# Edge gathers of a graph network kernel: one gather issued ahead of the wait for the preceding pair

## The chip, the core and the metric

The kernel runs on one core of one Trainium2 chip. Its time is the device time of one execution in microseconds; lower is better. "GB/s" and "us" below are those of the profile.

## The reference

One message passing layer with a residual and a layer norm, over 12,500 nodes of 64 features and 212,500 edges of 32 features, sorted by destination, all float32:

```python
msg_in = concatenate([nodes[row], nodes[col], edge_features])
messages = relu(msg_in @ mW1 + mb1) @ mW2 + mb2
aggregated = segment_sum(messages, col, num_segments=nodes.shape[0])
upd_in = concatenate([nodes, aggregated])
out = relu(upd_in @ uW1 + ub1) @ uW2 + ub2
result = layernorm(x + out)          # eps = 1e-5
```

`row` is the source of an edge, `col` its destination.

## The kernel before, in words

The source part of the message is linear ahead of the relu, so a first stage multiplies all nodes with the source rows of `mW1` and writes the product to a table in HBM, `table_src` (12,500 rows of 128 float32, 512 bytes each). The main loop then goes over the edges in 208 *pairs* p = 0 to 207. A pair is 1,024 edges in eight tiles of 128; the last is shorter. Each pair uses one of four slots, k = p mod 4, of every buffer. The sequence of a pair, by engine:

- **SyncE** (`load_two`, L636 and L639; `load_window`, L657) loads edge features (256 KB) and destination numbers, broadcast over 96 partitions (768 KB), for two pairs at a time, and a window of 96 destination nodes for each pair. A load waits for `pe_steps`, TensorE's count of steps that are over.
- **GpSimd** (`step`, L785 to L797) issues one indirect DMA for each tile: 128 rows of `table_src`, chosen by the source numbers in `idx_all`, 64 KB, into `gath` at slot k. Even pairs have eight gathers. Odd pairs from 11 on have seven: their eighth tile gets its source columns from ScalarE and VectorE instead (`col_x`, L516 and L539). Pairs 0 to 5 are gathered in another form, before the loop (L779). Each gather raises `gathered[k]` by 16 when it has landed.
- **TensorE** (`pre`, L912) multiplies the edges' features and a one-hot of their destinations into `ps_pre`; later (`summing`, L932) it adds the relu of the pair into the sums of 96 nodes, after which `window` (L845) prepares a window and ends the step (`pe_steps`).
- **VectorE** (`add_gathered`, L1298) adds `gath` to `ps_pre`, giving `hid`, and raises `hsum_made`; it waits for `pe_steps` and for `gathered[k]`. Its other work for a pair is the one-hots (L1261), `turned` (L1269) and the sums' ring (L1324, L1325).
- **ScalarE** takes the relu (L1103), copies 60 columns for each second pair (L516), and copies the window (L1065).

From pair 24 on, node work of 49 blocks of 256 nodes goes between, one block for four pairs (TensorE L979 to L995, ScalarE L1152 to L1160, VectorE L1402, output by L1164).

GpSimd's order is the program's own. Ahead of a pair's gathers `step` has up to four things: for p of 10 or more the wait that pair p-4 has been added (`hsum_made`, which frees the slot of `gath`), for p = 16 a wait for the rest of the index table, for p of 7 or more the wait that all gathers of pair p-1 have landed (`gathered[(k - 1) % SLOTS]`), and `let`, which raises a semaphore that nobody reads, so that the waits sit on an instruction of their own. `RAW` is 6, `SLOTS` 4, `EARLY` 16.

Of the kernel before, what the change touches and what calls it, by code (L numbers as in the profile page):

```python
# [41 lines left out]
SLOTS = 4  # L42
# [31 lines left out]
RAW = 6  # L74
# [46 lines left out]
def gnn_kernel(nc, x, xT, srcT, dst, dstT, edgeT, mW1, mb1, mW2T, mb2, uW1, ub1, uW2, ub2, out):  # L121
# [4 lines left out]
    with ExitStack() as ctx:  # L126
# [6 lines left out]
        def sem(name):  # L133
            return ctx.enter_context(nc.semaphore(name))
# [146 lines left out]
        gathered = [sem(f"gathered{i}") for i in range(SLOTS)]  # L281
# [44 lines left out]
        def let(eng):  # L326


            eng.sem_inc(passed, 1)
# [19 lines left out]
        def pair(it, k, back=0):  # L349

            it, k = it + (k - back) // SLOTS, (k - back) % SLOTS
            p = it * SLOTS + k
            return None if isinstance(p, int) and not 0 <= p < PAIRS else (p, it, k)

        def is_last(p):

            return isinstance(p, int) and p == LAST_PAIR
# [11 lines left out]
        def parts(p):  # L369

            return ((0, TILES, P), (TILES, 1, TAIL)) if is_last(p) else ((0, PT, P),)

        def tiles_of(p):

            return [(first + j, m) for first, t, m in parts(p) for j in range(t)]

        def rows_of(p):


            return LAST_ROWS if is_last(p) else PT  # L380
# [58 lines left out]
        def is_raw(p):  # L439

            return isinstance(p, int) and p < RAW
# [5 lines left out]
        def has_cols(p):  # L447

            return COL_FROM <= p < PAIRS and (p - COL_FROM) % COL_EVERY == 0
# [5 lines left out]
        def gathers_of(p):  # L455

            return rows_of(p) if is_last(p) else PT - has_cols(p)

        def got(p):


            return 16 * sum(gathers_of(q) for q in range(RAW, p + 1) if q % SLOTS == p % SLOTS)
# [87 lines left out]
        def src_by_tile(p, j, m):  # L550

            return bass.IndirectOffsetOnAxis(ap=idx_all[0:m, p * PT + j:p * PT + j + 1], axis=0)
# [198 lines left out]
        def _(pool):  # L751
# [33 lines left out]
            def step(it, k):  # L785
                p, it, k = pair(it, k)
                if is_raw(p):
                    return
                if p >= RAW + SLOTS:
                    pool.wait_ge(hsum_made, p - SLOTS + 1)  # L790
                if p == EARLY:
                    pool.wait_ge(idx_last_in, 16)
                if p > RAW:
                    pool.wait_ge(gathered[(k - 1) % SLOTS], got(p - 1))
                let(pool)
                for j, m in tiles_of(p)[0:gathers_of(p)]:
                    pool.indirect_dma_start(gath[0:m, k, j * H:(j + 1) * H], None, table_src, src_by_tile(p, j, m)).then_inc(gathered[k], 16)  # L797

            with pool.If(fit == 1):
                pool.wait_ge(idx_rest_in, 16)  # L800
                pairs(pool, step, lambda *chunk: None, lambda i: None)
# [698 lines left out]
```

## Time and profile before

| | |
|---|---|
| median of 3 runs | 2489.68 us (2489.13 to 2490.9) |
| the profiled execution | 2490.1 us |
| its span, first to last instruction | 2488.3 us |
| mean granted TensorE clock | 0.72 |
| busy: TensorE, GpSimd, VectorE, ScalarE | 62%, 59%, 45%, 39% |

The span is what the profile's rows cover; the time is 1.8 us more. In a group of instructions "busy" is the sum of their durations, and "idle" is how long their engine had nothing running before them, with what ended most of it. A releaser "issue" means that the profile shows nothing that the engine waited for; a GpSimd pause with that releaser can still be a wait, since semaphore instructions have no rows. A gather's duration is the generation of its descriptors, not the movement of its data.

### The profile page before, as it was taken

What the parts mean: (1) busy time and instruction counts of PE and PEld (TensorE: products, weight loads), DVE (VectorE), ACT (ScalarE), POOL (GpSimd) and SP (SyncE); (2) the same over time, 40 slices, a digit from 0 to 9 for tenths busy, and PEclk for the clock granted to TensorE, in tenths of its full rate; (3) what the DMA queues carried; (4) which work ended last, traced back from release to release, by engine and by line L of the source; (5) the groups of instructions that cost most, each with busy time, mean ns of one, the idle gap of its engine ahead of it and who ended that gap; (6) DMA issues with size and microseconds to landing.
All of it is one profiled execution on the core that took longest, in us unless ns stands there. A gap on an engine that the chain in (4) does not pass through costs nothing. (4 is left out here: it accounts for less than half of the span.)

```text
span 2488.3 us, 35326 instructions
## 1 busy us (share of the span) xinstructions
PE 1553.6 (62%) x8744; PEld 1428.1 (57%) x8744; DVE 1114.3 (45%) x4860; ACT 972.5 (39%) x6697; POOL 1475.7 (59%) x1576
## 2 busy tenths in 40 slices
PE   2676666665666666576666666567566566557657
PEld 2566655555565565565565565556566555556555
DVE  3435445444444444444444444444444444444443
ACT  1215334334334434443433433443433444443342
POOL 7155566666656666566666565665656666666653
PEclk6787776776766866766767777776766777676776
DMA  4634434333334333333333343343333343333331
GB/s 109 179 91 108 98 81 99 97 85 92 98 80 98 97 90 90 96 96 83 97 94 85 95 99 83 95 99 80 97 96 85 93 99 94 84 98 93 86 91 33
DMA packets 102736, 232.74 MB, mean 94 GB/s; under 512 B 47018, under 2 KB 63223, under 8 KB 89917
## 3 DMA queue, kind: packets, MB, share of 16 engines
q1 hardware_dynamic: 42532, 124.03, 19.9%
q0 software_dynamic: 49952, 100.83, 16.4%
q10 hardware_dynamic: 10046, 5.59, 0.9%
q8 instruction: 75, 1.23, 0.2%
q14 instruction: 131, 1.07, 0.2%
HBM read 220.66 MB, written 9.60 MB: 93 GB/s over the span
## 5 line engine op out<-in xcount | busy, mean ns | idle before, releaser
L797 POOL DMA_INDIRECT gath<-table_src,idx_all x1513 | 1427.6, 944 | 970.9 <-issue 873.0
L932 PE MATMUL ps_sum<-onehot,hid 128*128 128x96 f32 x3322 | 598.4, 353 | 628.0 <-ACT rhs L1065 535.8
L932 PEld LDWEIGHTS ps_sum<-onehot,hid 128*128 128x128 f32 x3322 | 563.4, 263 | 664.2 <-issue 659.8
L516 ACT COPY col_x<-xz 64x1 f32 x5960 | 634.9, 187 | 409.5 <-issue 403.9
L912 PE MATMUL ps_pre<-rhs,lhs 128*128 128x128 f32 x3226 | 593.7, 360 | 222.6 <-issue 164.3
L1298 DVE TENSOR_TENSOR hid<-ps_pre,gath 128x1024 f32<-128x1024 f32 x202 | 246.7, 1221 | 1067.3 <-DMA gath<-table_src,idx_all 925.6
L912 PEld LDWEIGHTS ps_pre<-rhs,lhs 128*128 128x128 f32 x3226 | 560.6, 270 | 244.1 <-issue 179.4
L1103 ACT ACTIVATE hid<-hid 128x1024 f32<-128x1024 f32 x202 | 212.7, 1053 | 358.9 <-DVE hid L1298 356.1
L539 DVE TENSOR_TENSOR col_x<-xz 64x2 int32 x3366 | 265.2, 148 | 81.5 <-issue 78.6
L1269 DVE TENSOR_SCALAR_CACHE_REDUCE lhs<-lhs,place 96x1024 f32<-96x1024 int32 x208 | 262.6, 1263 | 62.9 <-PE ps_sum L845 32.5
L1261 DVE TENSOR_TENSOR onehot<-ps_iota,dst_rel 128x768 f32<-128x768 f32 (+1 forms) x209 | 196.8, 942 | 0.1
L1065 ACT COPY rhs<-ps_sum 96x128 f32<-96x128 f32 x208 | 53.4, 258 | 307.6 <-issue 254.8
L1152 ACT ACTIVATE late_b<-ps_node,ub1c 128x256 f32<-128x256 f32 x47 | 22.3, 474 | 288.5 <-PE ps_node L985 270.1
L934 PE MATMUL ps_sum<-ident,deg 96*128 96x96 f32 x416 | 107.4, 350 | 2.5 <-issue 2.5
L845 PE MATMUL ps_sum<-w_dst,xwin 65*96 65x128 f32 x416 | 98.7, 324 | 9.7 <-DMA xwin<-in_xT_dram 9.7
L934 PEld LDWEIGHTS ps_sum<-ident,deg 96*128 96x128 f32 x416 | 89.1, 263 | 4.2 <-issue 4.1
L845 PEld LDWEIGHTS ps_sum<-w_dst,xwin 65*96 65x96 f32 x416 | 63.9, 189 | 23.3 <-DMA xwin<-in_xT_dram 10.1
L871 PE MATMUL ps_pre<-w_src,xz 128*128 128x128 f32 (+1 forms) x200 | 30.4, 321 | 60.4 <-ACT gath L1072 29.8
L871 PEld LDWEIGHTS ps_pre<-w_src,xz 128*128 128x128 f32 (+1 forms) x200 | 29.1, 231 | 61.2 <-issue 60.9
L1325 DVE TENSOR_TENSOR xz<-xz,ps_sum 1x96 f32 x208 | 54.2, 261 | 6.4
L919 PE MATMUL ps_pre<-w_src,col_x 64*128 64x128 f32 x200 | 53.4, 350 | 0.0
L1324 DVE TENSOR_TENSOR agg<-agg,ps_sum 128x96 f32 x208 | 50.6, 243 | 1.7 <-PE ps_sum L934 1.6
(136 smaller groups left out, 672.6 us busy)
## 6 DMA issues: line engine op xcount, KB each, us to landing
lhs<-in_dst_dram SPq DMA_DIRECT2D x99, 768.0 KB
lhs<-in_edgeT_dram SPq DMA_DIRECT2D x98, 256.0 KB
gath<-table_src,idx_all POOLq DMA_INDIRECT x1513
table_src<-gath SPq DMA_DIRECT2D x12, 512.0 KB, 5.3
xwin<-in_xT_dram SPq DMA_DIRECT2D x208, 24.0 KB
lhs<-in_dst_dram SPq DMA_DIRECT2D x10, 384.0 KB
out_dram<-late_b ACTq DMA_DIRECT2D x48, 64.0 KB, 2.7
xz<-in_xT_dram ACTq DMA_DIRECT2D x4, 512.0 KB, 5.1
```

The source lines that it names most:

```text
L516: ins = copy(col_x[:, k, start + n + j:start + n + j + 1], col)
L539: ins = nc.vector.tensor_tensor(to[:, at:at + 2].bitcast(I32), first, second, ALU.bitwise_or)
L797: pool.indirect_dma_start(gath[0:m, k, j * H:(j + 1) * H], None, table_src, src_by_tile(p, j, m)).then_inc(gathered[k], 16)
L845: return nc.tensor.matmul(win(p, k), xwin[:, k, :], w_dst[:, :], start=True, stop=True)
L871: mm = nc.tensor.matmul(ps_pre[q % 2][0:m, j * H:(j + 1) * H], xz[0:kk, of], w[0:kk, :], start=True, stop=True)
L912: mm = nc.tensor.matmul(to[0:m, j * H:(j + 1) * H], lhs[:, k, j * P:j * P + m], rhs[:, k, :], start=True, stop=not by_cols)
L932: nc.tensor.matmul(bank[:, 0:WIN], hid[0:m, k, j * H:(j + 1) * H], hot(k, j, m), start=(j == 0), stop=(m == TAIL or j == PT - 1))
L934: return nc.tensor.matmul(bank[:, P:P + WIN], deg[0:WIN, k:k + 1].broadcast_to([WIN, P]), ident[0:WIN, 0:WIN], start=True, stop=True)
L1103: nc.scalar.activation(h, h, ACT.Relu).then_inc(hid_made, 1)
L1261: ins = nc.vector.tensor_tensor(to, nums.broadcast_to([m, t, WIN]), at.broadcast_to([m, t, WIN]), ALU.is_equal)
L1269: nc.vector.tensor_scalar(whole, whole.bitcast(I32), place[0:WIN, cols(p, 1)], 0.0, ALU.is_equal, ALU.add, accum_out=deg[0:WIN, k:k + 1]). ...
L1298: nc.vector.tensor_tensor(hid[:, k, at], ps_pre[k % 2][:, at], gath[:, k, at], ALU.add).then_inc(hsum_made, 1)
```

## The change

In GpSimd's `step` the wait for pair p-1's gathers no longer stands ahead of the loop over the tiles but inside it, ahead of the second gather. An extra `let` goes with it.

```diff
@@ -790,10 +790,11 @@
                     pool.wait_ge(hsum_made, p - SLOTS + 1)
                 if p == EARLY:
                     pool.wait_ge(idx_last_in, 16)
-                if p > RAW:
-                    pool.wait_ge(gathered[(k - 1) % SLOTS], got(p - 1))
                 let(pool)
-                for j, m in tiles_of(p)[0:gathers_of(p)]:
+                for n, (j, m) in enumerate(tiles_of(p)[0:gathers_of(p)]):
+                    if n == 1 and p > RAW:
+                        pool.wait_ge(gathered[(k - 1) % SLOTS], got(p - 1))
+                        let(pool)
                     pool.indirect_dma_start(gath[0:m, k, j * H:(j + 1) * H], None, table_src, src_by_tile(p, j, m)).then_inc(gathered[k], 16)
```

The order of GpSimd's instructions at pairs 10 and 11 (slots 2 and 3), before:

```order
L797 DMA gath<-table_src,idx_all 128x128 [waits hsum_made,gathered1]
L797 DMA gath<-table_src,idx_all 128x128 x7
L797 DMA gath<-table_src,idx_all 128x128 [waits hsum_made,gathered2]
L797 DMA gath<-table_src,idx_all 128x128 x6
L797 DMA gath<-table_src,idx_all 128x128 [waits hsum_made,gathered3]
```

Each pair's first gather waits for both. The same place with the change:

```order
L798 DMA gath<-table_src,idx_all 128x128 [waits hsum_made]
L798 DMA gath<-table_src,idx_all 128x128 [waits gathered1]
L798 DMA gath<-table_src,idx_all 128x128 x6
L798 DMA gath<-table_src,idx_all 128x128 [waits hsum_made]
L798 DMA gath<-table_src,idx_all 128x128 [waits gathered2]
L798 DMA gath<-table_src,idx_all 128x128 x5
L798 DMA gath<-table_src,idx_all 128x128 [waits hsum_made]
```

The wait for the sums has stayed at the first gather, and the wait for the preceding pair's gathers is at the second. On the other engines nothing moves but line numbers, by one.

## Rows read from the trace of the kernel before

**Rows 1.** The page: its span, and section 1, busy time of each engine.

```profile
span 2488.3 us, 35326 instructions
...
PE 1553.6 (62%) x8744; PEld 1428.1 (57%) x8744; DVE 1114.3 (45%) x4860; ACT 972.5 (39%) x6697; POOL 1475.7 (59%) x1576
```

**Rows 2.** The page's costliest groups: busy, mean ns | idle before, releaser.

```profile
L797 POOL DMA_INDIRECT gath<-table_src,idx_all x1513 | 1427.6, 944 | 970.9 <-issue 873.0
...
L1298 DVE TENSOR_TENSOR hid<-ps_pre,gath 128x1024 f32<-128x1024 f32 x202 | 246.7, 1221 | 1067.3 <-DMA gath<-table_src,idx_all 925.6
```

**Rows 3.** Timeline of GpSimd, pairs 82 to 84: start, duration, work [idle before].

```profile
1011.41 0.95 POOL L797 DMA_INDIRECT gath<-table_src,idx_all  x1 [2.44 <-issue]
1012.66 0.94 POOL L797 DMA_INDIRECT gath<-table_src,idx_all  x1 [0.30 <-issue]
...
1020.17 0.94 POOL L797 DMA_INDIRECT gath<-table_src,idx_all  x1 [0.30 <-issue]
1023.44 0.94 POOL L797 DMA_INDIRECT gath<-table_src,idx_all  x1 [2.32 <-issue]
...
1034.28 0.94 POOL L797 DMA_INDIRECT gath<-table_src,idx_all  x1 [2.40 <-issue]
```

**Rows 4.** Timeline of other engines at the pause before pair 83.

```profile
1020.49 0.46 PE L845 MATMUL ps_sum<-w_dst,xwin 65*96 65x128 f32 x2
...
1022.77 1.23 DVE L1298 TENSOR_TENSOR hid<-ps_pre,gath 128x1024 f32<-128x1024 f32 x1 [6.23 <-DMA gath<-table_src,idx_all]
1022.93 0.32 SPq L636 DMA_DIRECT2D lhs<-in_edgeT_dram  x1
```

**Rows 5.** Timeline of GpSimd: first and last of 15 long pauses, pairs 33 and 201.

```profile
444.23 0.94 POOL L797 DMA_INDIRECT gath<-table_src,idx_all  x1 [4.58 <-issue]
...
2390.97 0.94 POOL L797 DMA_INDIRECT gath<-table_src,idx_all  x1 [4.57 <-issue]
```

**Rows 6.** Timeline of the early loop: pair 10's first gather, L1298 of pairs 11, 16.

```profile
170.19 0.94 POOL L797 DMA_INDIRECT gath<-table_src,idx_all  x1 [10.58 <-DVE hid L1298]
...
212.35 1.23 DVE L1298 TENSOR_TENSOR hid<-ps_pre,gath 128x1024 f32<-128x1024 f32 x1 [0.49 <-issue]
...
257.09 1.23 DVE L1298 TENSOR_TENSOR hid<-ps_pre,gath 128x1024 f32<-128x1024 f32 x1
```

**Rows 7.** Timeline of ScalarE over four pairs, without the column copies.

```profile
998.93 1.06 ACT L1103 ACTIVATE hid<-hid 128x1024 f32<-128x1024 f32 x1 [0.48 <-DVE hid L1298]
...
1010.97 0.25 ACT L1065 COPY rhs<-ps_sum 96x128 f32<-96x128 f32 x1
1012.00 1.06 ACT L1103 ACTIVATE hid<-hid 128x1024 f32<-128x1024 f32 x1 [0.79 <-DVE hid L1298]
...
1024.03 1.06 ACT L1103 ACTIVATE hid<-hid 128x1024 f32<-128x1024 f32 x1 [6.39 <-DVE hid L1298]
...
1035.97 1.06 ACT L1103 ACTIVATE hid<-hid 128x1024 f32<-128x1024 f32 x1
...
1045.91 0.47 ACT L1152 ACTIVATE late_b<-ps_node,ub1c 128x256 f32<-128x256 f32 x1 [6.09 <-PE ps_node L985]
```

**Rows 8.** Pauses that met a load, the loads, and two stretches (DMA share, GB/s last).

```profile
187.50 0.32 SPq L636 DMA_DIRECT2D lhs<-in_edgeT_dram  x1
...
196.57 0.94 POOL L797 DMA_INDIRECT gath<-table_src,idx_all  x1 [4.86 <-issue]
...
225.35 0.32 SPq L636 DMA_DIRECT2D lhs<-in_edgeT_dram  x1
...
233.65 0.95 POOL L797 DMA_INDIRECT gath<-table_src,idx_all  x1 [4.58 <-issue]
...
261.86 0.32 SPq L636 DMA_DIRECT2D lhs<-in_edgeT_dram  x1
...
270.57 0.94 POOL L797 DMA_INDIRECT gath<-table_src,idx_all  x1 [5.49 <-issue]
...
1000.00:1004.00 4.00, 3.00 (x26) 3.00 (x26) 2.63 (x20) 3.80 (x40) 2.83 (x3) 1.00 0.95 223
1006.00:1010.00 4.00, 0.00 (x0) 0.00 (x0) 0.00 (x0) 1.60 (x12) 2.37 (x3) 0.59 0.21 61
```

**Rows 9.** The chain that ended last: landing after the last gather.

```profile
2462.01 2.56 DMA gath<-table_src,idx_all
```

## The prediction

> **What bounds the kernel now.** I read the page first: its span and busy shares [rows 1]. No engine is near full: TensorE shows 62%, GpSimd 59%. So a wait sets the pace, and the costliest groups say which [rows 2]. VectorE's addition at L1298, the first reader of the gathered rows, spent 1067 us idle before its 202 instructions, 926 of them ended by the gathers' landing. GpSimd's own gathers, 1513 of 944 ns, had 971 us of idle time before them.
>
> The timeline of GpSimd shows how that idle time is made [rows 3]. Eight gathers of pair 82 start between 1011.41 and 1020.17, seven steps of 1.25 us (0.94 busy, 0.30 between). Then comes 2.32 us of nothing, and the first gather of pair 83 at 1023.44: 12.03 us from pair to pair. Pair 83 has seven gathers and takes 10.84 us (to 1034.28). The second half of the reading is who woke at that pause [rows 4]: the last gather is generated at 1021.12, VectorE's L1298, which waits for the same landing, starts at 1022.77, and GpSimd's next gather 0.67 us behind it. A pause is thus 1.65 us of landing and 0.67 us of restart; both are in the path, since GpSimd waits for the landing before it generates anything. The waits of pairs 7 to 207 are 201; 15 of them, every twelfth pair from 33 to 201, last 4.5 to 4.6 us [rows 5]. Their landing is on time and the restart is 2.2 us late; nothing in the profile says why.
>
> Is anything else as slow? At the start of the loop the gathers are far ahead, and the rest of the kernel runs at its own pace: L1298 of pair 11 at 212.35, of pair 16 at 257.09 [rows 6], so 8.95 us per pair. That is without the node work, which begins at pair 24. So from about pair 17 on, the gather stream bounds the loop with a margin of some 2.5 us per pair.
>
> **The change, part by part.**
>
> *The wait moves behind one gather.* For pair 83 the first gather would start 0.30 us after the last one of pair 82, at 1021.42, and be generated at 1022.37, still before the landing that L1298 sees at 1022.77. The second gather is then released by that landing and starts at 1023.44, where the first one started before. Each pair becomes shorter by one step, 1.25 us. The wait is still there, with about 1.1 us of it uncovered. This holds for the long pauses as well, as long as the pause is over 1.55 us; all are.
>
> *How many pairs count.* The first gather of pair 10 at 170.19 was released by L1298 of an earlier pair, not by a landing [rows 6]. That wait stays ahead of the first gather, so what is won before pair 10 is lost there. Pairs 11 to 207 remain: 197 x 1.25 = 246 us. From pair 11 to 16 the other engines are behind the gathers, and these savings do not show at once; they show when the others have caught up, since the gathers' own line of time keeps them.
>
> *Added instructions.* The wait for the sums used to sit with the wait for the gathers; now it stands alone, with a semaphore increment of its own. It is for the pair four back, whose L1298 was over some three pairs ago, so it waits for nothing. What an extra semaphore step costs has no row. Lower bound 0, since the gap of 0.30 us between gathers is there anyway; upper bound one such gap per pair, 197 x 0.30 = 59 us. I take 0: the 0.67 us of restart contain such a step already, and it now stands ahead of the first gather, where there is slack of 1.1 us before the landing's release.
>
> *What the earlier first gather touches.* Its slot was free since the wait for the sums passed. It puts 64 KB into the DMA queues behind the preceding pair's last gather, and its data moves after that one's. No instruction on SyncE or another queue moves. But the pairs get shorter, and SyncE's loads may meet other gathers. Where a load of 1,024 KB started 3 to 4 us before a pair's last gather was generated, the pause grew from 2.33 to 4.86, 4.58 and 5.49 us [rows 8], by 2.65 us in the mean and 3.16 at most. In steady state the load starts 0.16 us behind L1298 [rows 4], and nobody waits for the gathers that it meets. So a meeting costs between 0 and 3.16 us, and I take 0 for the sum, since the steady rows are the nearest; the rest is a rival.
>
> The Trainium skill (DMA: Bandwidth & Descriptors, "Queues, rings and completion order") says that each DMA engine takes turns between the queues that have work, packet by packet. By that rule a gather would wait for about one packet of the load; as an estimate, 16 x 8 KB at the 223 GB/s of [rows 8] is 0.6 us, and with one meeting in four pairs the time would be 2273. The trace does not agree: its pauses grew four times as much.
>
> *The 15 late restarts* cost 15 x 2.2 = 33 us now. They may fall elsewhere among the shifted instructions: between 0 and 33 us to gain, as much to lose. I take no change.
>
> *The tail.* From the last gather to the end (2462.01 to 2488.3) [rows 9] nothing changes.
>
> Sum: 2490.1 (the profiled execution's own time, 1.8 over its span) - 246 = 2244.1; the median of the runs is 0.4 lower, so 2244.
>
> **The rivals.**
>
> *ScalarE's chain takes over.* ScalarE copies columns for every second pair, and TensorE waits for its window copy (L1065) [rows 7]. From the relu at 998.93 to the next at 1012.00 it is idle for 0.79 us only: 12.3 us for a pair in which the gathers will leave 9.6. The pair after it needs 5.6 (12.0 less 6.4 idle), the next column pair 11.9 (1024.03 to 1035.97), and the fourth 10.4 to the end of L1152, which waits for TensorE. Together 40.2 us per four pairs, against 2 x (12.03 + 10.84) = 45.7 now and 45.7 - 5.0 = 40.7 after. So there is half a microsecond of slack in four pairs, and lateness in a column pair must be made up in the next. A chain longer by 1 to 1.5 us would cost 25 to 50 us over the 49 groups of four: about 2280. For it speaks the small slack, against it that TensorE's part was measured partly at half clock and that it would idle less.
>
> *The loads run into the last gather.* SyncE loads for every second pair, 98 times. TensorE's window matmul that frees the buffer ends at 1020.95, the load follows at 1022.93 [rows 4]. With pairs of 9.6 and 10.8 us the load of the pair behind a late ScalarE step (it came 11.7 us after the window copy's end at 1011.22) would start some 1 to 3 us before the next pair's last gather is generated. If one load of two collides, 49 x 2.65 = 130 us are given back: 2374. Against it speaks that the load keeps to the landing rather than to the matmul: 2 us pass between matmul and load, which no row explains.
>
> *All loads collide: slower.* The same mechanism at both loads of each four pairs. It decides at 246 / 98 loads = 2.5 us each. At 2.65 us the time is 2244 + 260 = 2504, at 3.16 it is 2554. It needs TensorE's steps to be out of step with the landings in both places. The second load would come to an end about 1 us before the last gather's data, by the same reckoning, so I hold this for unlikely.
>
> *Nothing is covered: no change.* If the landing were held up while GpSimd generates, the first gather would only push it back, and the time stays at 2490. Against it: with GpSimd generating and no load running the queues move 61 GB/s [rows 8], no less than the 52 GB/s of one gather's 64 KB per 1.25 us; so gathers land while others are generated.
>
> **How the numbers follow.** Forecast 2244: 0.52. ScalarE's chain, 2280: 0.14. One load of two, 2374: 0.26. All loads, 2504: 0.05. No change: 0.03. The low end takes the late restarts as gone, 2244 - 33 = 2211, and the high end reaches to the third case with its price at 3.16 (2244 + 155 = 2399, cut to 2395). A measurement of this kernel tells 0.2% (5 us) from no change. Faster by more: the first three, 0.92; within: 0.03; slower: 0.05.
>
> **What would show it.** Right: the pause moves between the first and second gather of a pair and is 1.1 us long, the step across the pair boundary is 1.25 us, two pairs take 20.4 us; L1298 still idles before the landing. The ScalarE rival shows as L1298 waiting for something other than the gathers; the load rivals as pauses of 3 to 4 us every fourth (or second) pair with an SP load starting before the last gather. I am wrong if the first gather of a pair is itself delayed, by the wait for the sums or by a longer generation than 944 ns.

## The result and the profile after

In the comparison the changed kernel takes 2838.13 us (median of 4 runs, 2819.52 to 2856.88) and the kernel before 2490.29 (4 runs): ratio 1.139 [1.132, 1.147], slower by 14%, far outside the range of the prediction. This verdict is one chip's. The same two kernels on another chip give 2197.68 against 2517.55, ratio 0.872 [0.868, 0.877]: faster by 13%. How these go together is what most of this text is about.

The page of the changed kernel, with the groups that answer to [rows 1, 2] (busy, mean ns | idle before, releaser), and its chain that ended last:

```profile
span 2855.2 us, 35526 instructions
...
PE 1579.5 (55%) x8744; PEld 1423.7 (50%) x8744; DVE 1134.0 (40%) x4860; ACT 1001.2 (35%) x6697; POOL 1478.1 (52%) x1576
...
another core or an unknown queue 43%; DVE 24%; issue 15%; PE 10%; DVEq 5%; ACT 1%; DMA 0%; SPq 0%; ACTq 0%
...
L798 POOL DMA_INDIRECT gath<-table_src,idx_all x1513 | 1429.9, 945 | 1307.3 <-DVE hid L1299 657.6
...
L516 ACT COPY col_x<-xz 64x1 f32 x5960 | 677.8, 190 | 720.7 <-issue 716.5
...
L1270 DVE TENSOR_SCALAR_CACHE_REDUCE lhs<-lhs,place 96x1024 f32<-96x1024 int32 x208 | 263.8, 1268 | 1298.2 <-remote 1204.0
...
L1299 DVE TENSOR_TENSOR hid<-ps_pre,gath 128x1024 f32<-128x1024 f32 x202 | 246.7, 1221 | 68.4 <-issue 57.0
```

Work has not grown: the gathers are 945 ns each as before, the busy sums are nearly those of [rows 1]. But the direction of waiting has turned. L1299 (before: L1298) idled 1067 us for the gathers [rows 2] and now 68; the gathers idle 1307 us instead of 971, half of it for VectorE's additions (`hid`, L1299), which free a slot of `gath`. VectorE in turn idles 1298 us ahead of `turned` (L1270), for something that the profile can only call remote, and the chain of waits is to 43% "an unknown queue". The kernel before had 63 us ahead of that instruction:

```profile
L1269 DVE TENSOR_SCALAR_CACHE_REDUCE lhs<-lhs,place 96x1024 f32<-96x1024 int32 x208 | 262.6, 1263 | 62.9 <-PE ps_sum L845 32.5
...
L516 ACT COPY col_x<-xz 64x1 f32 x5960 | 634.9, 187 | 409.5 <-issue 403.9
```

The second row, of the kernel before too, did not stand in the prediction and should have: ScalarE's column copies idled 404 us for nothing that the profile shows. Nor did the 44.6 us for which GpSimd idled ahead of the loop's first gather, at 109.07 us; they come up again below.

The timeline of the changed kernel, GpSimd:

```profile
1001.47 0.94 POOL L798 DMA_INDIRECT gath<-table_src,idx_all  x1 [0.30 <-issue]
...
1002.71 0.94 POOL L798 DMA_INDIRECT gath<-table_src,idx_all  x1 [0.30 <-issue]
...
1004.86 0.94 POOL L798 DMA_INDIRECT gath<-table_src,idx_all  x1 [1.20 <-issue]
...
1011.11 0.94 POOL L798 DMA_INDIRECT gath<-table_src,idx_all  x1 [0.30 <-issue]
...
1018.66 0.94 POOL L798 DMA_INDIRECT gath<-table_src,idx_all  x1 [6.61 <-DVE hid L1299]
...
1037.14 0.96 POOL L798 DMA_INDIRECT gath<-table_src,idx_all  x1 [8.79 <-DVE hid L1299]
```

The first pair boundary (1001.47, 1002.71, then the pause of 1.20 ahead of the second gather) is what the prediction drew. What it did not draw are the pauses of 6.6 and 8.8 us. The same stretch on the other engines:

```profile
1001.68 0.19 ACT L516 COPY col_x<-xz 64x1 f32 x1 [0.52 <-issue]
1001.68 0.15 DVE L539 TENSOR_TENSOR col_x<-xz 64x2 int32 x1 [0.56 <-issue]
1001.70 0.37 PE L846 MATMUL ps_sum<-w_dst,xwin 65*96 65x128 f32 x1 [1.86 <-issue]
1002.39 0.19 ACT L516 COPY col_x<-xz 64x1 f32 x1 [0.53 <-issue]
...
1003.09 0.19 ACT L516 COPY col_x<-xz 64x1 f32 x1 [0.51 <-issue]
1003.11 0.37 PE L846 MATMUL ps_sum<-w_dst,xwin 65*96 65x128 f32 x1 [1.05 <-issue]
...
1014.44 2.34 ACT L516 COPY col_x<-xz 64x1 f32 x24 [0.51 <-issue]
...
1014.88 1.27 DVE L1270 TENSOR_SCALAR_CACHE_REDUCE lhs<-lhs,place 96x1024 f32<-96x1024 int32 x1 [9.49 <-remote]
...
1016.65 1.23 DVE L1299 TENSOR_TENSOR hid<-ps_pre,gath 128x1024 f32<-128x1024 f32 x1
...
1019.64 3.81 ACT L516 COPY col_x<-xz 64x1 f32 x38
...
1024.71 0.46 PE L846 MATMUL ps_sum<-w_dst,xwin 65*96 65x128 f32 x2
...
1030.12 0.32 SPq L636 DMA_DIRECT2D lhs<-in_edgeT_dram  x1
```

ScalarE, VectorE and TensorE creep side by side, one instruction each per 0.71 us or a multiple of it, as if taking turns. TensorE's window matmuls (L846) end at 1003.48; VectorE's L1270, which waits for that step's count, starts 11.4 us later. Later the matmul ends at 1025.17 and the load that waits for the same count starts 4.95 us behind it. I call this the *hold*. It is over at 1014.44 (24 copies in 2.34 us, 0.10 each), some 2.4 us after the last gather that GpSimd could issue was generated (1012.05); the next one had to wait for L1299. After the restart at 1018.66 copies run at full speed until 1023.45; then the hold is back.

So it reads as a circle: the sums wait for TensorE's count, the count for a moment in which no gather is under way (I call it a *full stop*), and that moment often comes only when GpSimd has run out of free slots and stands waiting for the sums. In the kernel before every pair ended in such a full stop. There all 92 loads of edge features after 300 us start 1.74 to 1.99 us behind the end of a pair's last gather, which is its landing, and 0.6 to 3.6 us behind the matmul that releases them. With the change 59 of 93 start in a pause of GpSimd's, 30 held ones start while it generates, and 4 are prompt; the longest is 19.4 us behind its matmul. A full stop thus lets the count through, but it is not the only moment at which the count can pass.

### The profile page after: what moved, and what is told of

Read it like the earlier page. It is cut to its first block, busy times and chain, and to the rows that moved or that the text cites. A ratio compares the mean times of both kernels' runs of the same rounds, so it can differ in the third digit from the quotient of the medians.

```text
span 2855.2 us, 35526 instructions
## 1 busy us (share of the span) xinstructions
PE 1579.5 (55%) x8744; PEld 1423.7 (50%) x8744; DVE 1134.0 (40%) x4860; ACT 1001.2 (35%) x6697; POOL 1478.1 (52%) x1576
## 4 chain that ended last, share of the span: by engine, by line
another core or an unknown queue 43%; DVE 24%; issue 15%; PE 10%; DVEq 5%; ACT 1%; DMA 0%; SPq 0%; ACTq 0%
DVE col_x L539 8%; DVE hid L1299 7%; DVEq L500 4%; DVE onehot L1262 4%; PE ps_pre L913 4%; PE ps_sum L933 2%; DVE lhs L1270 2%; DVE xz L1326 1%; PE ps_sum L846 1%; DVE agg L1325 1%; ACT col_x L516 1%; DVEq L1309 1%; PE ps_pre L920 0%; DMA table_src<-gath 0%
## 5 line engine op out<-in xcount | busy, mean ns | idle before, releaser
L913 PE MATMUL ps_pre<-rhs,lhs 128*128 128x128 f32 x3226 | 618.2, 358 | 584.0 <-DVE lhs L1270 370.7
L516 ACT COPY col_x<-xz 64x1 f32 x5960 | 677.8, 190 | 720.7 <-issue 716.5
L1270 DVE TENSOR_SCALAR_CACHE_REDUCE lhs<-lhs,place 96x1024 f32<-96x1024 int32 x208 | 263.8, 1268 | 1298.2 <-remote 1204.0
L933 PE MATMUL ps_sum<-onehot,hid 128*128 128x96 f32 x3322 | 551.9, 331 | 329.5 <-ACT rhs L1066 149.3
L933 PEld LDWEIGHTS ps_sum<-onehot,hid 128*128 128x128 f32 x3322 | 522.7, 244 | 362.0 <-issue 305.6
L539 DVE TENSOR_TENSOR col_x<-xz 64x2 int32 x3366 | 280.7, 148 | 241.1 <-issue 239.2
L1299 DVE TENSOR_TENSOR hid<-ps_pre,gath 128x1024 f32<-128x1024 f32 x202 | 246.7, 1221 | 68.4 <-issue 57.0
L846 PE MATMUL ps_sum<-w_dst,xwin 65*96 65x128 f32 x416 | 110.4, 340 | 82.4 <-issue 72.3
L846 PEld LDWEIGHTS ps_sum<-w_dst,xwin 65*96 65x96 f32 x416 | 68.8, 197 | 96.4 <-issue 75.2
L995 PE MATMUL ps_node<-uw,late_b 128*128 128x64 f32 x188 | 48.2, 312 | 106.7 <-issue 106.7
L995 PEld LDWEIGHTS ps_node<-uw,late_b 128*128 128x128 f32 x188 | 44.1, 263 | 114.5 <-issue 114.4
L996 PE MATMUL ps_node<-cent,xz 65*128 65x64 f32 x188 | 50.3, 335 | 75.7 <-issue 75.7
L996 PEld LDWEIGHTS ps_node<-cent,xz 65*128 65x128 f32 x188 | 44.2, 267 | 86.2 <-issue 86.2
```

What stands on the lines that cost most here:

```text
L516: ins = copy(col_x[:, k, start + n + j:start + n + j + 1], col)
L539: ins = nc.vector.tensor_tensor(to[:, at:at + 2].bitcast(I32), first, second, ALU.bitwise_or)
L846: return nc.tensor.matmul(win(p, k), xwin[:, k, :], w_dst[:, :], start=True, stop=True)
L913: mm = nc.tensor.matmul(to[0:m, j * H:(j + 1) * H], lhs[:, k, j * P:j * P + m], rhs[:, k, :], start=True, stop=not by_cols)
L933: nc.tensor.matmul(bank[:, 0:WIN], hid[0:m, k, j * H:(j + 1) * H], hot(k, j, m), start=(j == 0), stop=(m == TAIL or j == PT - 1))
L1270: nc.vector.tensor_scalar(whole, whole.bitcast(I32), place[0:WIN, cols(p, 1)], 0.0, ALU.is_equal, ALU.add, accum_out=deg[0:WIN, k:k + 1]). ...
```

## The experiments

All but e8 and e9 compute the whole result; those two leave the source part out of the last pair's fourth tile. They ran on several chips; I name chip A (the kernel before at 2487 us) and chips B and C (2515 to 2518 us) by the number that came with each result. Chip A's runs lie before and between those of the others, so the hour of a run does not part them. The comparison above has no number, but its kernel before (2490 us) and its idle copies are those of chip A. The medians of e2 to e13 and of e15 are of two executions, the others of four to eight.

### Chip A: place and number of the full stops (e1 to e4)

e1 keeps the wait where it was and adds only the second `let`:

```diff
+                    if n == 1 and p > RAW:
+                        let(pool)
```

> The wait stays ahead of the first gather as before; only the extra semaphore increment ahead of the second gather is added. Theory P (what was lost is the full stop: a moment in each pair when GpSimd generates nothing and no gather is in flight, in which TensorE's step signals and the other engines' instructions get through): the full stop is there, so 2485 to 2505 us. Rival I (the extra semaphore instruction on GpSimd costs the time): near 2838.

2484.43 us, ratio 1.000 [0.998, 1.002]. The extra instruction costs nothing that can be told from noise.

e2 has a full stop in every pair, but one gather in. Against the kernel before:

```diff
-                if p > RAW:
-                    pool.wait_ge(gathered[(k - 1) % SLOTS], got(p - 1))
...
+                    if n == 1 and p > RAW:
+                        pool.wait_ge(gathered[(k - 1) % SLOTS], got(p - 1))
+                        pool.wait_ge(gathered[k], got(p) - 16 * (gathers_of(p) - 1))
+                        let(pool)
```

> The first gather goes ahead as in the change, but the second waits for it too, beside the preceding pair's gathers, so that nothing is in flight when it is released. Theory P: the full stop is back, one gather later, with the same length of 2.3 us, so about the time of before, 2480 to 2530 us. Rival C (the first gather of a pair, issued early, is itself what hurts, by contention with the last gathers or with the loads): still 2750 to 2850.

2462.33 us, ratio 0.990 [0.985, 0.995], a little below its range. One wait more than in the change, and 376 us less: rival C falls. The pauses are as long as before (2.23 to 2.64 us), but from 500 to 2300 us none is longer, where the kernel before has 13 of 4.4 to 4.7 us, the late restarts of [rows 5], and one of 3.2. The sum for all 15 late restarts was 33 us, the gain is 24.

e3 puts the wait of the change ahead of the fourth gather (`n == min(3, gathers_of(p) - 1)` in place of `n == 1`), e4 keeps it ahead of the first but in even pairs alone (`if p > RAW and p % 2 == 0`).

> The wait for the preceding pair stands ahead of the fourth gather, by when its gathers have long landed: no pause at all is left at the wait. Theory P: no full stop but those that the wait for the sums makes, so no better than the change: 2800 to 3000 us. Rival C by arithmetic of the gather stream (all of the 2.33 us pauses gone, 2030 us, plus at most 3.16 us for each of 98 loads): 2030 to 2400. Rival G (GpSimd's place in the sums' wait alone, the slots being too few for a stream that runs ahead): about 2838.

> The wait ahead of the first gather is kept for even pairs and left out for odd ones, so there is a full stop after every 15 gathers instead of every 7 or 8. Theory P: half of the stops are lost, TensorE's step signals come once in some 20 us, so slower than before: 2600 to 2850 us. The arithmetic of the gather stream (100 pauses of 2.33 us fewer): 2257 us.

e3: 2864.64 us, 1.152 [1.142, 1.161]. e4: 2767.16 us, 1.113 [1.107, 1.118]. Both wait less for landings than the kernel before, and both are slower, within the ranges of theory P. e3 alone does not part theory P from rival G, too few slots; e10 and e19 below do, which run ahead with the same four slots and are fast. ScalarE's copies, first e2, then e3, then e4:

```profile
L516 ACT COPY col_x<-xz 64x1 f32 x5960 | 635.6, 188 | 416.7 <-issue 412.5
```
```profile
L516 ACT COPY col_x<-xz 64x1 f32 x5960 | 655.7, 188 | 665.6 <-issue 663.4
```
```profile
L516 ACT COPY col_x<-xz 64x1 f32 x5960 | 662.1, 188 | 680.5 <-issue 678.8
```

Three kernels with a full stop in each pair (before, e1, e2) take 2462 to 2487 us, the three that have none or have it in every second pair only (the change, e3, e4) 2767 to 2865.

### Chip B: a pause in place of the wait, and no columns (e5, e6, e8, e9)

e6 takes the wait away and makes a pause in which gathers stay under way (`STOPS = 1`); e5 is the same with `STOPS = 3`:

```diff
-                    pool.wait_ge(gathered[(k - 1) % SLOTS], got(p - 1))
+                    for r in range(STOPS):
+                        nc.gpsimd.memset(scratch[:, :], 0.0).then_inc(stops, 1)
+                        pool.wait_ge(stops, (p - RAW - 1) * STOPS + r + 1)
```

> No wait for landed gathers at all; between two pairs GpSimd instead clears a scratch tile three times, each time waiting for itself, about 3 us in all. It thus generates nothing for longer than the 1.65 us that a landing takes, but waits for no gather. Theory P (a moment with nothing generated and nothing in flight is what counts): as before, only with the longer stop, 2490 + 197 x (3.0 - 2.3) = about 2630 us, 2550 to 2720. Rival W (it is the wait for the landing itself that counts, for instance because it holds GpSimd's sequencer back): 2800 or more, as in the run with the wait ahead of the fourth gather.

> The same with one clearing, a pause of about 1.2 us, in which the last gather is still in flight (it lands 1.65 us after it was generated). Theory P in its strict form (nothing may be in flight): slow, 2700 to 2870 us. Theory G (it is enough that nothing is being generated for a microsecond): near the arithmetic of the gather stream, 2490 - 197 x 1.1 = 2270 us, up to 2400.

e5: 2456.22 us, 0.976 [0.974, 0.979]. e6: 2223.69 us, 0.884 [0.881, 0.887]. Both are faster than any theory had them. e5's median pause is 2.49 us, longer than a landing of 1.65, so it still has a full stop; e6's is 1.32 us, so e6 has none. There is no hold in either. Two rows of e6's GpSimd and its page's row of the copies:

```profile
1006.87 0.55 POOL L798 MEMSET scratch<- 128x512 f32 x1
1008.21 0.95 POOL L802 DMA_INDIRECT gath<-table_src,idx_all  x1 [0.79 <-POOL scratch L798]
```
```profile
L519 ACT COPY col_x<-xz 64x1 f32 x5960 | 562.6, 187 | 4.5 <-issue 2.2
```

5 us in place of 404 to 717. I took this to refute the full stop. That was hasty: I had not looked at the kernel before that ran beside it, which had gone from 2487 to 2517 us.

e8 and e9 leave the column path out (`has_cols` returns False; ScalarE gets one wait for the column table near the end), so that all pairs have eight gathers and the copies are gone; e8 has the wait of the kernel before, e9 that of the change.

> The kernel before without the column path: all pairs but the last have eight gathers, ScalarE and VectorE copy no columns for them (the last pair's fourth tile lacks its source part, which changes that part of the result). The stream of gathers sets the time: 99 gathers of 1.25 us more, 2490 + 124 = 2614 us; ScalarE and VectorE have some 9,000 instructions fewer. It is the base of the next run.

> The change without the column path (leaves out the same as the run before). If the loss comes from TensorE's step signals alone, held while gathers are generated or in flight, the copies do not matter and it is 8 to 16% slower than its base, 2800 to 3000 us. If it comes from the many small instructions of ScalarE and VectorE competing with the gathers, the loss is gone, and the time is its base less 197 x 1.25 = 246 us, about 2370.

2838.69 and 2670.97 us, each far from what was expected: the change is worth 168 us here, not 246. The gathers' rows of e8 and e9:

```profile
L797 POOL DMA_INDIRECT gath<-table_src,idx_all x1611 | 1520.9, 944 | 1226.6 <-issue 1154.9
```
```profile
L798 POOL DMA_INDIRECT gath<-table_src,idx_all x1611 | 1521.2, 944 | 1054.6 <-DMA gath<-table_src,idx_all 550.6
```

The idle time falls by 172 us. e8 is far over what was expected since its pauses are long: 66 of 143 between 500 and 2300 us are over 3 us. All 66 have a load that started 2.8 to 4.7 us before the pair's last gather was generated, and their landings are late, as shown below for e14. e9 has 16 late restarts like those of [rows 5], which e8 has not; they are 35 us of what the change falls short by.

### Chip B again: is it the wait, or GpSimd's instructions? (e10 to e13)

e10 has neither wait nor memset:

```diff
-                if p > RAW:
-                    pool.wait_ge(gathered[(k - 1) % SLOTS], got(p - 1))
```

Nothing computed needs the wait: a slot is written only after the sums of the pair four back, and its reader waits for the slot's own count. e11 is e6 with a `scratch` of 8 columns in place of 512. e12 has wait and memset ahead of the first gather, e13 the memset there and the wait of the change ahead of the second.

> GpSimd issues all its gathers with no wait for earlier gathers and nothing else between pairs (the wait for VectorE's sums of the pair four back stays). Theory A, that GpSimd's standing wait on the gathers' own semaphore is what holds the other engines back, as the pair of busy runs (no such wait, fast) suggests: as fast as the run with one short memset or a little faster, since the 1 us beside the memset goes too, 2050 to 2250 us. Theory B, that gathers issued back to back with no instruction of GpSimd's own between them let its sequencer run ahead and keep the other engines' signals out, and that the memset was what cured it: as slow as the changed kernel or slower, 2800 to 2950 us, with VectorE's and TensorE's instructions 0.7 us apart in the middle of a pair.

> The run with one short memset, the memset 8 columns wide in place of 512 (still waited for by GpSimd itself). Theory B: the cure is the instruction and its wait, not its length, so the pause shrinks from 1.3 to 0.8 to 1.0 us and the time falls from 2224 to 2140 to 2215 us if GpSimd is the bound. If a pause of some minimal length is what the other engines need, or if the memset's own length was the cure: slower than 2224, up to 2850 us.

> The kernel before, with the memset and its wait put behind the wait for the preceding pair's gathers, both ahead of a pair's first gather. Theory A (the standing wait does the harm): no better than before, and 0.5 to 1 us per pair longer, 2560 to 2700 us. Theory B (a GpSimd instruction of its own between pairs cures): the pause is 2.3 + 0.5 to 1.0 us but TensorE's steps are prompt and nothing restarts late, so it goes by the gathers alone, 7.5 x 1.245 + 2.5 to 3.0 us per pair, 2440 to 2560 us.

> The changed kernel with one short memset and its wait ahead of a pair's first gather, the wait for the preceding pair's gathers still ahead of the second. Theory A: the standing wait is there, so as slow as the changed kernel, 2780 to 2900 us. Theory B: the memset restores the others, so near the run with the memset alone: 2230 to 2420 us (by then the preceding pair's gathers have landed 1.3 us earlier, and the wait at the second is short or none).

e10: 1981.31 us, 0.787 [0.777, 0.797]. e11: 2138.61, 0.849 [0.842, 0.856]. e12: 2831.78, 1.125 [1.113, 1.136]. e13: 2249.61, 0.893 [0.885, 0.901]. The gathers and the copies of e10, then the memset and the copies of e12:

```profile
L795 POOL DMA_INDIRECT gath<-table_src,idx_all x1513 | 1427.8, 944 | 461.7 <-issue 455.0
...
L516 ACT COPY col_x<-xz 64x1 f32 x5960 | 562.4, 188 | 4.0 <-issue 2.2
```
```profile
L519 ACT COPY col_x<-xz 64x1 f32 x5960 | 563.0, 187 | 5.3 <-issue 2.2
...
L800 POOL MEMSET scratch<- 128x512 f32 x201 | 105.4, 525 | 617.3 <-DMA gath<-table_src,idx_all 617.3
```

e10 refutes theory B as stated and e12 theory A: it has the standing wait and no hold. Neither theory's range holds e12's time. That is its longer pause alone (4.60 us in the mean against 3.01 in e14, times 201 pairs = 320 us; measured 313): 0.66 us of it is the memset, 133 us in all, and the rest is loads, of which all 66 between 500 and 2300 us start shortly before a pair's last gather is generated. e10 is bound by generating: 1513 x (0.944 + 0.305) = 1889 us, with 65 us ahead of the first gather of the loop and 30 behind the last. Its 76 loads between 500 and 2300 us all start 0.03 us behind their matmul, though generation never pauses.

### Chip C: one difference at a time (e14 to e17)

e14 is the kernel before with the buffer and the semaphore of e6 declared and never used:

```diff
+        scratch = sb("scratch", [P, 512])
...
+        stops = sem("stops")
```

e15 is e12 with a `let` between the wait and the memset. e16 is the kernel before without GpSimd's `let(pool)`, e17 with `pool.sem_inc(pool_passed, 1)` in its place, a semaphore of GpSimd's own.

> The kernel before with the scratch buffer and the semaphore of the memset runs declared but never used. If where the buffers and semaphores lie did the cure in e12: ScalarE's column copies lose the 404 us of idle time, and the time leaves 2490 us by more than 1%. If it is an instruction of GpSimd's that matters: same as before, ratio 1.00, the copies idle 380 to 420 us.

> e12 with one instruction more: the increment of the shared semaphore 'passed' stands directly behind the wait for the preceding pair's gathers and carries it, as in the kernel before; then the memset, its wait and the gathers. Theory C, that an increment that itself stands on the gathers' semaphore is what holds the others: held as before, ScalarE's column copies idle about 400 us. Theory D, that it is the gather directly behind the wait: the memset stands between them here, so not held, 5 us of idle and 2780 to 2880 us as e12.

> The kernel before without the increment of 'passed' ahead of GpSimd's gathers; both waits stand on no increment. Theory C: the others are free (column copies idle about 5 us) while the pause stays at 2.3 us; the time by the gathers alone is then 2400 to 2500 us, or that of e12 less its memset, about 2700, if free engines make the gathers land later. Theory D: held as before, 2490 us, idle about 400 us.

> The kernel before with GpSimd's increment going to a semaphore of its own instead of the one that all engines increment. Theory E, that the shared semaphore is the meeting point: the others are free, column copies idle about 5 us. Theories C and D: no difference, 2490 us, ratio 1.00, idle about 400 us.

2520.46 us, 1.001 [0.998, 1.004]; 2835.36, 1.129 [1.119, 1.139]; 2504.00, 0.996 [0.992, 0.999]; 2516.65, 1.002 [0.999, 1.005]. None of this can decide between theories C, D and E: the copies idle 5 us in all four, e14 included, which does what the kernel before does. There was no hold for any of them to end. The gathers, the copies and two other rows of e14:

```profile
L799 POOL DMA_INDIRECT gath<-table_src,idx_all x1513 | 1427.6, 944 | 996.7 <-issue 938.3
...
L518 ACT COPY col_x<-xz 64x1 f32 x5960 | 562.7, 187 | 5.0 <-issue 2.2
```
```profile
1009.62 0.74 PE L847 MATMUL ps_sum<-w_dst,xwin 65*96 65x128 f32 x2
1010.39 0.32 SPq L638 DMA_DIRECT2D lhs<-in_edgeT_dram  x1
```

The load follows the matmul's end by 0.03 us, with the pair's last gather generated only 0.3 us before and not landed; on chip A it took 1.98 [rows 4]. That an unused buffer should do this is hard to believe; what else had changed with every kernel since e5 was the chip.

### The changed kernel on chips A and B (e18, e19)

Unaltered.

> The changed kernel once more, unaltered, beside the kernel before. Theory F, that the hold belongs to the surroundings of the run and not to the kernel (the unused buffer of e14 can hardly have cured it): if the kernel before reads about 2515 us here, ScalarE's column copies idle about 5 us in place of 717, nothing waits 7 to 10 us for VectorE's sums, and the time comes out near the run with the memset and the wait ahead of the second gather (2250 us), 2150 to 2350 us; if the kernel before reads about 2488 us, it is held again and 2820 to 2860 us. Theory G, that the hold goes with the kernel's own code and layout: 2820 to 2860 us whatever the kernel before reads, the copies idle about 700 us.

> The changed kernel once more, unaltered. Theory F (the hold belongs to the chip): where the kernel before reads about 2515 us, the column copies idle about 5 us and the time is 2150 to 2350 us, by what the same edit with a memset ahead gave (2250 us) and the prediction's sum (2244 us). Theory G (the hold belongs to the kernel, and the chip's number is chance): 2760 to 2860 us with idle copies where the kernel before reads 2515 us too. Theory H: the copies are free but the wait ahead of the second gather still lets late sums in, 2400 to 2700 us. Where the kernel before reads about 2488 us the run tells nothing new: 2760 to 2860 us.

e18 ran on chip A: 2776.77 us beside 2487.54, ratio 1.116 [1.109, 1.122], the copies idle 677 us. e19 ran on chip B, beside a kernel before of 2517.55 us: 2197.68, ratio 0.872 [0.868, 0.877]. Its page:

```profile
span 2201.4 us, 35526 instructions
...
L798 POOL DMA_INDIRECT gath<-table_src,idx_all x1513 | 1427.8, 944 | 682.1 <-issue 402.8
...
L1299 DVE TENSOR_TENSOR hid<-ps_pre,gath 128x1024 f32<-128x1024 f32 x202 | 246.6, 1221 | 933.9 <-DMA gath<-table_src,idx_all 905.4
...
L516 ACT COPY col_x<-xz 64x1 f32 x5960 | 562.4, 188 | 4.0 <-issue 2.0
...
L1270 DVE TENSOR_SCALAR_CACHE_REDUCE lhs<-lhs,place 96x1024 f32<-96x1024 int32 x208 | 262.6, 1262 | 27.8 <-PE ps_sum L846 15.2
```

and a pair boundary in its timeline:

```profile
999.30 0.94 POOL L798 DMA_INDIRECT gath<-table_src,idx_all  x1 [0.30 <-issue]
...
999.79 0.56 PE L846 MATMUL ps_sum<-w_dst,xwin 65*96 65x128 f32 x2
...
1000.38 0.32 SPq L636 DMA_DIRECT2D lhs<-in_edgeT_dram  x1
1000.63 1.22 DVE L1299 TENSOR_TENSOR hid<-ps_pre,gath 128x1024 f32<-128x1024 f32 x1 [4.86 <-DMA gath<-table_src,idx_all]
...
1001.30 0.94 POOL L798 DMA_INDIRECT gath<-table_src,idx_all  x1 [1.06 <-DMA gath<-table_src,idx_all]
...
1002.96 5.12 ACT L516 COPY col_x<-xz 64x1 f32 x53
```

Theory F stands. The same program gives 2777 to 2838 us with the hold and 2198 without; L1299 waits for the gathers again, the copies take 0.10 us each with gathers under way, the pause is 1.06 us. e18 lies below the range that was set for the held case (2820 to 2860).

The gain, 320 us, is more than the 246 of the prediction. The page has it: the gathers' idle time falls from 996.7 (e14) to 682.1, 315 us. From 500 to 2300 us the mean pause falls from 3.01 us (149 pauses, 48 over 3 us) to 1.38 (161, 10 over 3 us). Three things make up the 315. All 201 waits lose a step here, none being for a slot: 251 us. The 15 late restarts of [rows 5] are in e14 too and not in e19: 33 us. The rest, some 30, is meetings with loads: from 300 us on, late landings cost 74 us in e14 and 47 in e19. Two long pauses of e14, each with its load, VectorE's start and GpSimd's restart:

```profile
533.29 0.32 SPq L638 DMA_DIRECT2D lhs<-in_edgeT_dram  x1
534.72 1.22 DVE L1300 TENSOR_TENSOR hid<-ps_pre,gath 128x1024 f32<-128x1024 f32 x1 [6.23 <-DMA gath<-table_src,idx_all]
537.59 0.94 POOL L799 DMA_INDIRECT gath<-table_src,idx_all  x1 [4.54 <-issue]
```
```profile
1104.25 0.32 SPq L638 DMA_DIRECT2D lhs<-in_edgeT_dram  x1
1107.85 1.23 DVE L1300 TENSOR_TENSOR hid<-ps_pre,gath 128x1024 f32<-128x1024 f32 x1 [7.81 <-DMA gath<-table_src,idx_all]
1110.72 0.94 POOL L799 DMA_INDIRECT gath<-table_src,idx_all  x1 [6.21 <-issue]
```

In the first the landing is on time (VectorE starts 1.66 us behind the last gather's generation) and the restart 2.2 us late. In the second both are late: 3.34 us to VectorE's start and 2.87 from there. In 43 of e14's 48 long pauses a load started between 5 us before the end of the pair's last gather and 0.32 behind it; a landing then takes up to 4.07 us, and where it takes 1.6 the pause is long by its late restart alone. In all ten of e19 the load started two microseconds before.

On chip A none of the kernel before's 78 loads of that time starts in those 5 us; they start with the landing, as shown above. There the steady stretch passes 155 pauses, of 2.53 us in the mean, in the time of e14's 149. That is, as I read it, why the kernel before is faster on chip A by 30 us: the hold spares it the meetings. All its pauses together are 70 us shorter than e14's. It gives 44 of them back ahead of the loop's first gather, which starts at 109 us there and at 65 in e14.

## Why the prediction failed

- **The wait moves behind one gather, 1.25 us per pair: right on both chips.** The gather ahead of the wait starts 0.3 us behind its predecessor, and the median pause behind it is 1.13 us on chip A (as far as no slot is waited for) and 1.11 on the other, forecast 1.1. On chip A the waits for slots then take back more than this gives.
- **The added instruction, no longer generation: right.** e1 puts the instruction at 0 within some 5 us (upper bound 59 us); a gather stays at 944 or 945 ns. **Pairs that count: 201 in place of 197** on chips B and C, where pair 10 does not wait for a slot.
- **"What the earlier first gather touches" is the step that failed.** It said that no instruction on SyncE or another queue moves, and it gave a price only to meetings of loads and gathers. On chip A the full stop at the end of each pair was what let TensorE's count, and with it VectorE, SyncE and ScalarE, go on. One gather ahead of the wait takes it away: VectorE idles 1298 us ahead of L1270 in place of 63, GpSimd's gathers idle 336 us more, and the time rises by 348 us in place of falling by 246. The step reckoned the wait as 2.33 us of lost time only, and not as the moment that others needed.
- **The clue was in the text.** The prediction noted that "2 us pass between matmul and load, which no row explains" and used it as evidence against a rival. The same trace has the 404 us of the column copies. Both show other engines late for nothing that the profile names: of the copies between 500 and 2300 us, 4 of 2,918 in the first four microseconds behind GpSimd's restart have idle time of over 0.3 us ahead, and 485 of 1,088 in the next six. A rival in which a pair without the stop is held longer would have followed; its size could not have been told from these rows.
- **The loads' term was taken at 0 from rows of chip A**, where load and gather keep apart. Without the hold they do meet, and the change gains some 30 us by meeting less often. The rivals of the loads had the right mechanism with the wrong sign. So e19's 2198 us lies below the range too: 251 of its 320 us are the mechanism of the prediction, the rest are two terms that it put at 0.
- **The estimate of 0.6 us for a meeting was too small.** e19's ten pauses of 3.00 to 5.50 us against 1.11 put it at 1.9 to 4.4. The Trainium skill (DMA: Bandwidth & Descriptors, "Queues, rings and completion order") says that a DMA engine takes turns packet by packet, and that a packet has typically 9 to 17 descriptors; the estimate took one transfer of 8 KB per engine for a packet. So the measurement decides against that size, and not against the rule.
- **ScalarE's chain did not take over.** In e19 L1299 idles 934 us for the gathers, and e10 shows that the other engines keep up at 1981 us. The slack worked out from [rows 7] was too small; those rows hold a part of the 404 us that the copies idled on chip A, which I take for the reason.
- **The 15 late restarts** were taken as unchanged, with 33 us as the most to gain. They are gone in e2 (24 us) and in e19. They are no part of the hold: in e12 and e14 to e17, free of it, the same 15 gathers restart as late, 2.2 us each. What they hang on, the runs don't show.

What stays open: what the hold is, and whether the chip itself has it or something that stays beside that chip; also why the changed kernel reads 2838 in the comparison and 2777 in e18. That e5 to e13 and e15 were free of it because of their chip rests on e14, e16, e17 and e19 beside [rows 2] and e18; e10, the fastest, was not run on chip A. By e3 and e4, which stop seldom there, it may well be slow on that chip. The only edit that was faster on chip A is e2, by 1.0%. That a full stop ends the hold is read from the timelines and from the six kernels of chip A, e2 beside the change above all.

## What to carry to other kernels

A wait is not only lost time: before it is taken away, look at what the other engines do during it, and above all for rows of idle time with the releaser "issue" and for a count that arrives late. An effect that the rows show on every engine at once (instructions in step, 0.71 us apart) calls for a run on a second chip before any theory of the kernel. And the kernel before, run beside each experiment, is data: its move from 2487 to 2517 us, from e4 to e5, told of the chip long before I read it.

## What the chips showed that I had not expected

- On one chip, while indirect gathers are generated and land, ScalarE, VectorE and TensorE issue about one instruction per 0.71 us. In the kernel before this begins some 4 us after the gathers' restart, and TensorE's count reaches SyncE 0.6 to 3.6 us late; in the changed one up to 19.4. On the others the same instructions run at full speed (copies 0.10 us apart), and the count is seen 0.03 us after the matmul's end.
- One program, 2777 to 2838 us on one chip and 2198 on another. The sign of the change depends on it.
- Without any wait between pairs GpSimd generates 1513 gathers one per 1.25 us to the end, and the kernel takes 1981 us, a fifth less than before on that chip.
- Where a 1,024 KB load starts while a pair's last gathers are generated, VectorE, which waits for the last one's landing, starts as much as 4.07 us (e14), 4.82 (e19) and 6.12 (e12) after its generation, in place of 1.65.
- GpSimd restarts 2.2 us late at the same 15 gathers, 90 apart, on three chips (before, e1, e12, e14 to e17), and in e9 at 16 gathers, 96 apart: every twelfth pair each time. In e2, e8, e10, e13 and e19 no such restart is seen in the steady stretch.
